# V with a ones column per head, loaded whole and masked in place by ScalarE: one edit to a fused vision kernel

## What is computed

```python
xn = _layernorm(x, norm1_w, norm1_b)
qkv = (xn @ qkv_w.T + qkv_b).reshape(Bx, Nx, 3, H, hd).transpose(2, 0, 3, 1, 4)
q, k, v = (qkv[0], qkv[1], qkv[2])
attn = jax.nn.softmax(jnp.einsum('bhqd,bhkd->bhqk', q, k) * scale, axis=-1)
o = jnp.einsum('bhqk,bhkd->bqhd', attn, v).reshape(Bx, Nx, C)
x = x + (o @ proj_w.T + proj_b)
```

## Time and profile before

| | |
|---|---|
| median of 3 runs | 420.41 us (418.99 to 421.50) |
| the profiled execution, its own time | 418.79 us |
| its span in the trace | 417.0 us |
| mean granted TensorE clock | 0.894 |
| TensorE busy | 324.6 us, 78% |
| VectorE busy | 251.0 us, 60% |
| ScalarE busy | 140.0 us, 34% |
| GpSimd busy | 93.3 us, 22% |

### The profile page before, as it was taken

How to read it: one execution, slowest core, us unless ns; L and a number is a source line. 1 busy time by engine, 2 the same in 40 slices (tenths; PEclk the granted TensorE clock), 3 DMA queues, 4 the chain that set the end, 5 groups by cost and what they waited for, 6 DMA issues and landing times.

```text
span 417.0 us, 6118 instructions
## 1 busy us (share of the span) xinstructions
PE 324.6 (78%) x2039; PEld 289.1 (69%) x2039; DVE 251.0 (60%) x585; ACT 140.0 (34%) x328; POOL 93.3 (22%) x89
## 2 busy tenths in 40 slices
PE   4998338229996588999978977636669999999990
PEld 4988226218884466988866765525659999999990
DVE  1454999988697997534976478558823332223230
ACT  0043545019241226353362614313033333333330
POOL 9320100041001001000110000002522555544631
PEclk9999859658997889999998989965859999999997
DMA  8930000000000101423222454710041223222321
GB/s 277 368 96 1 0 0 2 0 0 1 2 1 0 25 8 32 116 49 97 74 75 27 121 153 125 221 52 2 0 134 22 38 40 43 43 48 40 45 26 20
DMA packets 31786, 25.27 MB, mean 61 GB/s; under 512 B 18146, under 2 KB 26802, under 8 KB 31754
## 3 DMA queue, kind: packets, MB, share of 16 engines
q1 hardware_dynamic: 27866, 20.82, 17.9%
q0 software_dynamic: 3888, 4.03, 6.5%
HBM read 20.12 MB, written 4.72 MB: 60 GB/s over the span
## 4 chain that ended last, share of the span: by engine, by line
PE 46%; DVE 31%; issue 6%; SPq 5%; ACT 4%; DMA 4%; POOL 3%; DVEq 0%; ACTq 0%; POOLq 0%
PE banks L1435 9%; PE banks L1424 7%; PE banks L1426 7%; PE banks L1228 5%; PE banks L1251 5%; PE banks L1229 4%; SPq L521 4%; PE banks L1298 4%; DVE arena L959 3%; POOL rs L577 2%; DVE patch L1004 2%; PE banks L1349 2%; DVE xh L892 1%; DVE st L864 1%; DVE patch L1142 1%
## 5 line engine op out<-in xcount | busy, mean ns | idle before, releaser
L577 POOL TENSOR_TENSOR rs<-va,consts 96x6 f32<-96x6 f32 (+1 forms) x16 | 21.5, 1344 | 239.9 <-DVE va L870 153.0
L609 POOL DMA_INDIRECT out<-s,ffn x20 | 31.8, 1588 | 51.0 <-DVE s L1192 48.3
L1192 DVE TENSOR_SCALAR s<-banks,ffn 128x192 f32<-128x192 f32 x20 | 8.4, 418 | 57.0 <-PE banks L1435 56.8
L1435 PE MATMUL banks<-arena,ffn 128*128 x240 | 42.1, 326 | 0.0
L817 ACT ACTIVATE ffn<-banks 128x384 f32<-128x384 f32 x40 | 19.6, 491 | 62.2 <-PE banks L1426 62.2
L1435 PEld LDWEIGHTS banks<-arena,ffn 128*128 128x128 f32 x240 | 38.5, 190 | 0.0
L1261 PE MATMUL banks<-consts,xh 96*128 96x96 f32 (+1 forms) x96 | 12.8, 277 | 30.0 <-DVEq L894 30.0
L1261 PEld LDWEIGHTS banks<-consts,xh 96*128 96x128 f32 (+1 forms) x96 | 10.2, 143 | 32.8 <-DVEq L894 31.9
L1251 PE MATMUL banks<-arena,patch 128*96 128x192 f32 x144 | 26.9, 351 | 5.6 <-DMA patch<-in_xp 5.6
L1251 PEld LDWEIGHTS banks<-arena,patch 128*96 128x96 f32 x144 | 25.5, 178 | 6.5 <-DMA arena<-in_tokw 5.6
L1298 PE MATMUL banks<-rvw,ffn 128*96 128x192 f32 x144 | 25.5, 327 | 1.3 <-ACT ffn L738 1.3
(11 more groups left out here) (216 smaller groups left out, 764.4 us busy)
## 6 DMA issues: line engine op xcount, KB each, us to landing
arena<-in_w SPq DMA_DIRECT2D x8, 576.0 KB, 5.3
...
arena<-in_w1a SPq DMA_DIRECT2D x8, 384.0 KB, 4.4
...
vs<-v_scratch SPq DMA_DIRECT2D x96, 9.0 KB
v_scratch<-vt SPq DMA_DIRECT2D x4, 216.0 KB, 2.2
xh_scratch<-xh SPq DMA_DIRECT2D x4, 216.0 KB, 2.3
...
```

Source lines behind the costliest of these rows:

```text
L577: pool.tensor_tensor(dst, src, const_("power", T)[:, 0:n * GTILES], ALU.pow).then_inc(rstd_ready, 1)
L609: pool.indirect_dma_start(out[:, :], bass.IndirectOffsetOnAxis(ap=IS[:, j:j + 1], axis=0), YG[j % 2], None, compute_op=ALU.add).then_inc(s ...
L1435: ins = mm(ps[:, 0:C], HST[j % 2][:, 128 * k:128 * (k + 1)], W2[:, bass.ds(e, 1), C * k:C * (k + 1)], start=(k == 0), stop=(k == HB - 1))
```

## The change

`VT`, the scratch tensor and `VS` now hold V with 17 columns per head: 16 channels and a one. GpSimd sets the ones in `VT` once. A half is loaded by three transfers, one for each block of 36 partitions, and each carries whole rows of all 12 heads (204 columns, 816 bytes), 4 images at once. `VS` then holds every head in every block, and a new step `vm:half:g` on ScalarE multiplies, in place, the columns of each of the three heads of a slab by a column of the constant `slab`, which is one in the partitions of that head and zero elsewhere: three instructions per half. TensorE's `pv` waits for these three and no longer for the load. GpSimd's clearing of `VS` goes. `pv` and `weighted` follow the new places of the columns.

```diff
@@ -32,7 +32,8 @@
 NH, HD = 12, 16
 HS = 3
 NS = NH // HS
-SW = HS * HD + HS
+HW = HD + 1
+SW = HS * HW
 E = 8
 MT = (2 * TOK + E * 127) // 128
...
@@ -242,9 +242,9 @@
         SHIFT = sb("shift", [T, TILES])
         QT = sb("qt", [128, 2, 2, GT + 32])
         KT = sb("kt", [128, 2, GT])
-        VT = sb("vt", [T, GTILES, C])
+        VT = sb("vt", [T, GTILES, NH, HW])
         vs_ = sb("vs", [128, GI * NS * SW])
-        VS = vs_[0:HS * NT, :].rearrange("p (i s c) -> p i s c", i=GI, s=NS)
+        VS = vs_[0:HS * NT, :].rearrange("p (i c) -> p i c", i=GI)
         S = sb("s", [128, 2, NH * NT])
         MX = sb("mx", [128, 2, NH])
         RI = sb("ri", [128, 2, NH])
@@ -281,7 +281,8 @@
         ke_ready = sem("ke_ready")
         v_stored = [sem(f"v_stored{g}") for g in range(G)]
         v_loaded = [sem(f"v_loaded{i}") for i in range(2 * G)]
-        vs_cleared = sem("vs_cleared")
+        v_masked = [sem(f"v_masked{i}") for i in range(2 * G)]
+        ones_set = sem("ones_set")
         nb_ready = sem("nb_ready")
         xh_scaled = sem("xh_scaled")
         p_ready = sem("p_ready")
@@ -443,7 +444,7 @@
         HST = [fcarve(HID) for _ in range(2)]
         WE = [x.rearrange("p (b n) -> p b n", b=2) for x in (rvw[:, :], fcarve(2 * HID))]
 
-        v_dram = nc.dram_tensor("v_scratch", [TOK, C], F32).ap()
+        v_dram = nc.dram_tensor("v_scratch", [TOK, NH * HW], F32).ap()
         xh_dram = nc.dram_tensor("xh_scratch", [TOK, C], F32).ap()
 
         block = ctx.enter_context(nc.Block())
@@ -505,20 +506,20 @@
                                  XH[:, GTILES * (g % 2):GTILES * (g % 2 + 1), :]).then_inc(xh_stored[g], 16)
                 if kind == "vt":
 
+                    sp.wait_ge(ones_set, 1)
                     for t in group_tiles(g):
                         taken(sp, ("vt", t))
-                    sp.dma_start(v_dram[GT * g:GT * (g + 1), :].rearrange("(t p) c -> p t c", p=T), VT[:, :, :]).then_inc(v_stored[g], 16)
+                    sp.dma_start(v_dram[GT * g:GT * (g + 1), :].rearrange("(t p) c -> p t c", p=T),
+                                 VT[:, :, :, :].rearrange("p t h x -> p t (h x)")).then_inc(v_stored[g], 16)
                 if kind == "vl":
                     half = step[1]
                     sp.wait_ge(v_stored[g], 16)
                     if g:
                         full(sp, ("pv", GI // 2 * (g - 1) + 2 * half + 1))
-                    if g == 0 and half == 0:
-                        sp.wait_ge(vs_cleared, 1)
-                    src = v_dram[GT * g:GT * (g + 1), :].rearrange("(i t) (s h d) -> h t i s d", t=NT, s=NS, h=HS)
+                    images = slice(4 * half, 4 * half + 4)
+                    src = v_dram[GT * g:GT * (g + 1), :].rearrange("(i t) c -> t i c", t=NT)[:, images, :]
                     for h in range(HS):
-                        for i in range(4 * half, 4 * half + 4):
-                            sp.dma_start(VS[NT * h:NT * (h + 1), i, :, HD * h:HD * (h + 1)], src[h, :, i, :, :]).then_inc(v_loaded[2 * g + half], 16)
+                        sp.dma_start(VS[NT * h:NT * (h + 1), images, :], src).then_inc(v_loaded[2 * g + half], 16)
                 if kind == "wo":
                     wo_seen += 1
                 if kind == "pt" and wo_seen == G:
@@ -559,11 +560,7 @@
             ch.step(pool.memset(WOWODD[0:C1, :], 0.0))
             pool.sem_inc(weights_cleared, 1)
             ch.step(pool.memset(OT[C1:C1 + 1, :, 1, :], 1.0))
-            ch.step(pool.memset(VS[:, :, :, :], 0.0))
-            pool.wait_ge(loaded["const"], 16)
-            ones = const_("slab", HS * NT)[:, 0:HS * HD].rearrange("p (h d) -> p h d", h=HS)[:, :, 0]
-            pool.tensor_copy(VS[:, :, :, HS * HD:SW].rearrange("p i s h -> p (i s) h"),
-                             bc(ones.unsqueeze(1), [HS * NT, GI * NS, HS])).then_inc(vs_cleared, 1)
+            pool.memset(VT[:, :, :, HD:HW], 1.0).then_inc(ones_set, 1)
 
             nstat = 0
             for step in STEPS:
@@ -760,7 +757,14 @@
                         act.wait_ge(v_stored[g - 1], 16)
                     for i, t in enumerate(group_tiles(g)):
                         ps = full(act, ("vt", t))
-                        freed(A(VT[:, i, :], ps[0:T, 0:C], ACT.Copy), ("vt", t))
+                        freed(A(VT[:, i, :, 0:HD], ps[0:T, 0:C].rearrange("p (h d) -> p h d", h=NH), ACT.Copy), ("vt", t))
+                if kind == "vm":
+
+                    half = step[1]
+                    act.wait_ge(v_loaded[2 * g + half], 16 * HS)
+                    for h in range(HS):
+                        v = VS[:, 4 * half:4 * half + 4, :].rearrange("p i (s x) -> p i s x", s=NS)[:, :, :, HW * h:HW * (h + 1)]
+                        A(v, v, ACT.Copy, scale=const_("slab", HS * NT)[:, HD * h:HD * h + 1]).then_inc(v_masked[2 * g + half], 1)
                 if kind == "exp":
                     p = step[1]
                     taken(act, ("s", p))
@@ -1014,16 +1018,14 @@
                 freed(TTR(e, ps, bc(MX[:, p % 2, :].unsqueeze(2), [128, NH, NT]), ALU.subtract), ("s", p))
 
             def weighted(p):
-                ps = full(dve, ("pv", p))[:, 0:2 * NS * SW].rearrange("p (a s c) -> p a s c", a=2, s=NS)
-                ri = RI[:, p % 2, :].rearrange("p (s h) -> p s h", s=NS)
-                ch.step(dve.reciprocal(ri, ps[:, 0, :, HS * HD:SW]))
+                ps = full(dve, ("pv", p))[:, 0:2 * NS * SW].rearrange("p (a h x) -> p a h x", a=2, x=HW)
+                ch.step(dve.reciprocal(RI[:, p % 2, :], ps[:, 0, :, HD]))
                 if p >= 2:
                     full(dve, ("ot", p - 2))
                 for a in range(2):
                     r = slice(64 * a, 64 * a + 64)
-                    ins = TTR(O[r, p % 2, :].rearrange("p (s h d) -> p s h d", s=NS, h=HS),
-                              ps[r, a, :, 0:HS * HD].rearrange("p s (h d) -> p s h d", h=HS),
-                              bc(ri[r].unsqueeze(3), [64, NS, HS, HD]), ALU.mult)
+                    ins = TTR(O[r, p % 2, :].rearrange("p (h d) -> p h d", h=NH), ps[r, a, :, 0:HD],
+                              bc(RI[r, p % 2, :].unsqueeze(2), [64, NH, HD]), ALU.mult)
                 freed(ins, ("pv", p))
 
             def proj(g):
@@ -1342,11 +1344,12 @@
                     ps = begin(("pv", p))
                     taken(pe, ("pt", p))
                     gg, q = divmod(p, GI // 2)
-                    pe.wait_ge(v_loaded[2 * gg + q // 2], 16 * HS * GI // 2)
-
-                    po = ps[:, 0:2 * NS * SW].rearrange("p (a s c) -> p a s c", a=2, s=NS)
+                    pe.wait_ge(v_masked[2 * gg + q // 2], HS)
+
+                    po = ps[:, 0:2 * NS * SW].rearrange("p (a c) -> p a c", a=2)
                     for s in range(NS):
-                        ins = mm(po[:, :, s, :], PT[:, p % 2, 128 * s:128 * (s + 1)], VS[:, 2 * q:2 * q + 2, s, :], start=True, stop=True)
+                        ins = mm(po[:, :, SW * s:SW * (s + 1)], PT[:, p % 2, 128 * s:128 * (s + 1)], VS[:, 2 * q:2 * q + 2, SW * s:SW * (s + 1)],
+                                 start=True, stop=True)
                     end(ins, ("pv", p))
                 elif kind == "ot":
                     p = g
```

More of the change, by code:

```diff
@@ L95 @@
-rv:1 turn:2:1 rv:2 wkv:1:4 ff:0 kf:0:1 kf:1:1 hx:1 wkv:1:5 stats:b:0 apply:b:0 rv:3 rv:4 rv:5 ff:1 wkv:1:6
-turn:b:0 qk:0 vt:0 vl:0:0 stats:b:1 spread:0 apply:b:1 wo:2 wo:3 turn:b:1 s:0 s:1 vt:1 exp:0 pt:0 stats:2:2
-vl:1:0 apply:2:2 qk:1 exp:1 stats:2:3 turn:2:2 apply:2:3 s:2 spread:1 hx:2 kf:0:2 kf:1:2 pt:1 s:3 rv:6 exp:2
-exp:3 pv:0 pv:1 hx:3 vl:0:1 rv:7 turn:2:3 ot:0 pt:2 pt:3 rv:8 pv:2 s:4 ot:1 pv:3 ot:2 vl:1:1 kf:0:3 ot:3 kf:1:3
-proj:0 stats:g:0 ff:2 exp:4 rv:9 apply:g:0 rv:10 stats:b:2 s:5 turn:g:0 apply:b:2 base:0 rv:11 pt:4 logits:0
@@ L100 @@
-pv:4 exp:5 s:6 pt:5 ot:4 s:7 pv:5 ff:3 turn:b:2 stats:b:3 qk:2 exp:6 vt:2 spread:2 ot:5 vl:0:2 exp:7 pt:6 pv:6
-pt:7 s:8 exp:8 pv:7 ot:6 apply:b:3 vl:1:2 ot:7 proj:1 stats:g:1 turn:b:3 s:9 qk:3 apply:g:1 pt:8 vt:3 s:10 exp:9
-exp:10 pv:8 pt:9 s:11 ot:8 pt:10 turn:g:1 exp:11 pv:9 vl:0:3 pv:10 ot:9 pt:11 ot:10 logits:1 pv:11 base:1
-spread:3 ot:11 vl:1:3 proj:2 s:12 s:13 stats:g:2 exp:12 pt:12 exp:13 apply:g:2 pt:13 pv:12 s:14 turn:g:2 pv:13
-ot:12 exp:14 logits:2 s:15 pt:14 exp:15 ot:13 pt:15 pv:14 pv:15 ot:14 ot:15 proj:3 base:2 stats:g:3 base:3
@@ new lines @@
+wo:1 wexp:1:3 wexp:1:4 stats:2:1 kf:0:0 hx:0 kf:1:0 apply:2:1 wkv:1:3 rv:0 rv:1 turn:2:1 rv:2 wkv:1:4 ff:0 kf:0:1
+kf:1:1 hx:1 wkv:1:5 stats:b:0 apply:b:0 rv:3 rv:4 rv:5 ff:1 wkv:1:6 turn:b:0 qk:0 vt:0 vl:0:0 stats:b:1 spread:0
+apply:b:1 wo:2 wo:3 turn:b:1 s:0 s:1 vt:1 exp:0 pt:0 stats:2:2 vl:1:0 apply:2:2 qk:1 exp:1 stats:2:3 turn:2:2
+apply:2:3 s:2 spread:1 hx:2 kf:0:2 kf:1:2 pt:1 s:3 rv:6 exp:2 exp:3 vm:0:0 pv:0 pv:1 hx:3 vl:0:1 rv:7 turn:2:3 ot:0
+pt:2 pt:3 rv:8 vm:1:0 pv:2 s:4 ot:1 pv:3 ot:2 vl:1:1 kf:0:3 ot:3 kf:1:3 proj:0 stats:g:0 ff:2 exp:4 rv:9 apply:g:0
@@ new lines @@
```

(6 more changed lines are left out.)

10 lines of the change are left out of this document (4 added, 6 removed).

## The result

The changed kernel takes 451.95 us (median of 4 runs, 451.57 to 453.54), the kernel before 420.96 us (median of 4, 418.99 to 428.60). The ratio is 1.076, with a 95% interval of 1.0708 to 1.0812: slower by 31 us. It has the direction and half of the size.

A forecast was written before the change was run, and what follows sets the result against it. It took TensorE's own order, fed by ScalarE's evictions and exponentials and by VectorE, as the bound; delays at pv summed to 15.0 us on 418.8, 433.8, or 435.4 us as a median, range 428.5 to 441.

The forecast's parts named there:

- The cost of a mask: On ScalarE, 24 new mask instructions of 511 ns each, 1.33 us for the three of a half, 10.6 us in all.
- The loads: On SyncE, 96 V transfers become 24, 1.2 us of issue per half instead of 9.6; gain 0.83 us before pv:10.
- The bound of 4.4 us for the landing: A half's 352 KB of V lands between 2.2 and 4.4 us, the latter the time of a 384 KB weight load.
- The pauses: In the attention stage, TensorE stands before the first pv of each half until ScalarE's late masks end.
- The sum of 15.0 us: Delays at the pv matmuls, each passed on in full to the experts' stage, added to the time before.
- the term of the sum for TensorE's clock: Slower TensorE work after the new pauses; left out of the sum, so counted as 0.
- the second rival: Same pauses, plus one or two more falls of TensorE's clock at 1.7 us each: 437 to 441 us; chance 0.17.
- dense work: Argument against more clock falls: the new TensorE pauses are mostly single and surrounded by dense work.
- Absorption: Rival 3: unseen slack behind the stalls takes up part, half of 15 us giving 427.9 us; chance 0.13.
- rival 4: ScalarE has time to spare, masks don't delay TensorE, only 0.83 us is gained: 419.6 us; chance 0.05.
- rival 5: SyncE's queue paces the attention stage, and 8.4 us of issue drop out: 412.0 us; chance 0.03.
- What would show it: Trace signs: 24 short load issues, 24 masks, TensorE waits at pv, experts' stage equally long, starting some 15 us later.

The follow-up runs named there:

- masks_early: The changed kernel with its eight mask steps moved forward to places where ScalarE waits for others; 425.59 us, ratio 1.004.
- masks_late_filled_half: The changed kernel with 4 to 14 dummy identity matmuls on TensorE in each pause before a half's first pv; 435.32 us, ratio 1.0356.
- masks_placed: masks_early with the two masks that waited for their loads moved back to ScalarE gaps between load and use; 417.57 us, ratio 0.9917.

## Why the prediction was wrong, step by step

- **The cost of a mask.** Forecast 511 ns each and 1.33 us for three, worked out from ScalarE's groups; measured 520 ns and 1.36 us. Right, 0.2 us over the eight.
- **The loads.** Forecast 0.4 us an issue, 1.2 for a half; measured 0.39 and 1.15 to 1.17, once 1.45. Right. The bound of 4.4 us for the landing was too low for a load with weights just ahead of it: 6.5 us in masks_early. In the changed kernel it made no difference, since its masks stand so late that they never waited for a load.
- **The pauses.** Forecast as waits, by place: 2.79, 1.89, 1.13, 2.36 (with the 1.16 already there), 3.26, 1.94 (with the 0.83), 2.10, 2.10. Measured: 2.74, 1.83, 1.10, 2.46, 3.30, 2.05, 2.03, 2.03. Each is within 0.11 us. The sum of 15.0 us was right within 1.5 as well: with TensorE kept busy during the pauses, masks_late_filled_half came out with a span 16.5 us over that before. That its 435.32 us meet the forecast of 435.4 so closely is partly luck, since 0.8 us of late start and some remaining loss of clock are in it, and it ran on another chip.
- **The step that failed is the term of the sum for TensorE's clock.** The text said "I leave it out of the sum and make it the second rival", and that rival counted the falls as "once or twice more", at 1.7 us each. The chip had a fall behind seven of the eight pauses. Together they made 17 us (450.4 less 433.5 us of span), where the sum had 0 and the second rival 3.4. The mechanism was named, and its number and size were not worked out. The price of 1.7 us was right for the shortest falls (pv:0 and pv:4); the other five lasted longer and lost 3.4 to 6.6 us. The count came from a guess about "dense work" around the pauses. Against that guess stood a row that was not read: the kernel before has a second fall of the same size (0.88 and 0.69 from 244 to 252 us), again behind short pauses (1.20 and 0.81 us). And pv:4 shows that dense work ahead of a pause didn't keep the clock up.
- **Rivals 3 to 5.** Absorption was slight: 13.7 us more idle time between 170 us and pv:14, for 15.5 us of new waits. That the masks hide (rival 4) is what masks_early and masks_placed have, at other places. SyncE's queue paced nothing (rival 5): with 96 loads and the same masks the time was the same, 452.42 against 451.95 us.
- **What would show it.** The prediction said that the experts' stage would be as long as before and start 15 us later. It is as long (112.5 us), and starts 33.5 us later.
